# Dilated attention: router steps dealt over the heads, row copies on ScalarE, contexts in halves, the second router's root by Newton steps

## The reference, cut to what matters

```python
# dilated attention: 16 heads of 8 channels; segments of 256, 512 and the last 16 tokens,
# with dilation 1, 2, 4 (a head sees every r-th token of its segment in a Hilbert order)
s = einsum('bhqd,bhkd->bhqk', qd, kd) * SCALE;  p = softmax(s);  od = einsum('bhqk,bhkd->bhqd', p, vd)
t = t + o @ w_out + b_out
# the last mixture: routing on the layer-normed token
x = (t - mean) / sqrt(var + 1e-5);  gate_logits = x @ gate_weight.T
top_vals, top_idx = top_k(gate_logits, 2);  routing_w = softmax(top_vals)
# h_sum per expert, h_mean, y_mean = h_mean @ w2;  out = sum_k routing_w * y_mean[top_idx]
```

## Time and profile before

| | |
|---|---|
| median of the runs | 3198.56 us (3 runs, 3196.73 to 3207.51) |
| profiled execution | 3192.41 us, span 3190.6 us |
| busy over the span | PE 2720.5 us (85%), DVE 2120.3 (66%), ACT 1553.2 (49%), POOL 996.4 (31%) |
| mean granted TensorE clock | 0.92 |
| dilated stage, scores and finish | from 2040 us (first score) to 2822 us of the span |

### The profile page before, as it was taken

One profiled execution on the slowest core, in us unless ns is written; L12 is line 12 of the kernel. 1 busy time (PEld: TensorE's weight loads), 2 busy tenths in 40 slices (PEclk: granted clock), 3 DMA queues, 4 the chain that ended last, 5 costly groups with the idle time before them and its releaser, 6 DMA issues. The chain is left out here.

```text
span 3190.6 us, 63614 instructions
## 1 busy us (share of the span) xinstructions
PE 2720.5 (85%) x21060; PEld 1483.0 (46%) x21061; DVE 2120.3 (66%) x3976; ACT 1553.2 (49%) x3278; POOL 996.4 (31%) x1323
## 2 busy tenths in 40 slices
PE   8988799999999999999399889688888888728887
PEld 4545143333333434333299768354555554413334
DVE  6745777877777777774222268767777777646665
ACT  2246366666666666666155434444544444404442
POOL 0024011222222222222333474235655655630000
PEclk9989599999999999999699989788898898859998
DMA  2036522322223222220222234433232232032223
GB/s 87 1 122 228 80 38 41 57 47 43 43 48 53 52 43 43 44 43 9 90 62 62 69 121 159 100 54 60 59 65 60 59 65 60 24 121 61 60 59 118
DMA packets 209456, 215.90 MB, mean 68 GB/s; under 512 B 33280, under 2 KB 185152, under 8 KB 209216
## 3 DMA queue, kind: packets, MB, share of 16 engines
q1 hardware_dynamic: 180880, 175.22, 23.8%
q0 software_dynamic: 14336, 25.72, 3.0%
q10 hardware_dynamic: 14000, 11.73, 1.3%
HBM read 129.23 MB, written 81.90 MB: 66 GB/s over the span
## 5 line engine op out<-in xcount | busy, mean ns | idle before, releaser
L1544 ACT ACTIVATE attn_exps<-attn_sbank 128x392 f32<-128x392 f32 x1600 | 704.8, 504 | 466.3 <-PE attn_sbank L1461 461.5
L1589 DVE TENSOR_REDUCE attn_mx<-attn_rot 128x1 f32<-128x784 f32 x768 | 722.1, 967 | 187.4 <-PE attn_rot L1474 184.3
L2315 ACT ACTIVATE dil_exps<-dil_sbank 128x512 f32<-128x512 f32 x512 | 289.4, 598 | 364.4 <-PE dil_sbank L2213 361.2
L1474 PE MATMUL attn_rot<-attn_k,attn_q 96*128 96x392 bf16 x1536 | 402.0, 345 | 71.1 <-DVE attn_mx L1589 40.5
L1461 PE MATMUL attn_sbank<-attn_q,attn_k 99*128 99x392 bf16 x1536 | 450.5, 333 | 11.0 <-ACT attn_exps L1544 9.7
L2371 DVE TENSOR_REDUCE dil_mx<-dil_rot 128x4 f32<-128x1024 f32 x256 | 307.5, 1218 | 72.9 <-PE dil_rot L2223 70.7
L1501 PE MATMUL attn_acc<-attn_exps,attn_v 128*32 128x392 f32 x3584 | 349.8, 501 | 0.0
L1461 PEld LDWEIGHTS attn_sbank<-attn_q,attn_k 99*128 99x128 bf16 x1536 | 148.9, 98 | 269.3 <-ACT attn_exps L1544 134.7
L2704 PE MATMUL silu_ph<-silu_route_w,silu_xT 128*128 x424 | 238.2, 646 | 37.6 <-DVE silu_xT L2754 19.2
L1474 PEld LDWEIGHTS attn_rot<-attn_k,attn_q 96*128 96x128 bf16 x1536 | 117.8, 99 | 277.6 <-DVE attn_mx L1589 180.4
L2223 PE MATMUL dil_rot<-dil_k,dil_q 96*128 96x256 bf16 x1024 | 176.5, 302 | 75.5 <-DVE dil_mx L2371 49.5
(11 more groups left out here) (389 smaller groups left out, 4517.8 us busy)
## 6 DMA issues: line engine op xcount, KB each, us to landing
attn_q<-q_pieces SPq DMA_DIRECT2D x192, 98.0 KB, 3.5
attn_k<-k_pieces SPq DMA_DIRECT2D x192, 98.0 KB, 4.7
silu_x<-silu_rows SPq DMA_DIRECT2D x212, 64.0 KB, 1.7
dil_q<-dil_q_pieces SPq DMA_DIRECT2D x192, 66.0 KB
dil_k<-dil_k_pieces SPq DMA_DIRECT2D x192, 66.0 KB
q_pieces<-qkv_piece SPq DMA_DIRECT2D x16, 588.0 KB, 3.1
k_pieces<-qkv_piece SPq DMA_DIRECT2D x16, 588.0 KB, 4.2
v_rows<-qkv_v SPq DMA_DIRECT2D x16, 476.0 KB, 3.8
```

The source lines that it names most:

```text
L1474: ins = nc.tensor.matmul(rot[b][:, hf, 0:HS], q[nxt.side][g][0:QROWS, j, c * P:(c + 1) * P], k_[nxt.side][g][0:QROWS, j, cols], start=True ...
L1544: nc.scalar.activation(e_[:, n % NP, :], sbank[(n + t.side) % 3][:, 0:HS], ACT.Exp, scale=A_DIM ** -0.5).then_inc(s_ex, 1)
L1589: nc.vector.tensor_reduce(into, rot[b][:, :, 0:HS], AX.XY, ALU.max).then_inc(s_free, 1)
L2315: nc.scalar.activation(e_[:, k % NP, :], sbank[k % 3][:], ACT.Exp, scale=D_DIM ** -0.5).then_inc(s_ex, 1)
```

## The change

- Root: `act_root`, its square root on ACT and the reciprocal go; the two-picks router calls `dve_rsqrt`, as the first router does (a shift, a scaled negative, a first guess and three Newton rounds of three instructions, 12 on 112x7). The picks become 15 steps: in each, one step of the search for the best two and one of the norm go out together, after a wait for both of the step before.
- Copies: rows and gate are copied out of PSUM by ACT (`act_rows`, `act_gate`), as steps in ACT's list.
- `s_free` becomes one semaphore for each of the two `rot` banks, since two engines free them now.
- Contexts: `weigh` is dealt in halves (group, segment), 16 products each, at score units 8g+6 and 8g+10; `take` at 8g+12 (from 8g+13). An exponential that reuses a slot waits for the half that read it.
- Order: picks 0 to 9 at heads 11 to 15, two a head; picks 10 to 14 at heads 0 to 2 of the next turn (lag 2); ranks and soft at 3; places over heads 4 to 9; gate 10, store 11; scatters at heads 7 to 15 (2, 2, 1, 2, 1, 2, 1, 2, 1), at the end of a head; compact 3, den 5, add 7, rows 9; turn 0 at 10. POOL's norm comes at pick 13, in head 1 of the next turn.

```diff
-        self.ROOT = 2 + 2 + 3 * NEWTON if K == 1 else 9
-        self.PICKS = self.ROOT + 8 if K == 1 else 16
+        self.RSQRT = 2 + 3 * NEWTON
+        self.ROOT = 2 + self.RSQRT if K == 1 else 2 + self.RSQRT
+        self.PICKS = self.ROOT + 8 if K == 1 else self.ROOT + 2
...
+    def act_rows(self, act, im, rot):
+        nc, E = self.nc, self.ex.n
+        im.wait(act, self.s_xt, lambda e: e)
+        im.wait(act, self.s_cs, lambda e: self.PLACE_LINKS * (e - 1) + 4 if e else 0)
+        nc.scalar.activation(self.xc[:, 0:4, :], rot[0:TOK, 0, :].rearrange("k (c d) -> k c d", c=4), ACT.Copy)
+        nc.scalar.activation(self.xc[:, 4:NCH, :], rot[0:TOK, 1, 0:3 * P].rearrange("k (c d) -> k c d", c=3), ACT.Copy).then_inc(self.s_xc, 1)
+        return nc.scalar.activation(self.raw[:], rot[0:TOK, 1, 3 * P:3 * P + NCH * E].rearrange("k (c e) -> k c e", e=E), ACT.Copy)
...
     def dve_picks_two(self, dve, im):
+        ch = Links(dve, self.s_ch, self.PICK_LINKS * im.e, self.PICK_LINKS)
+        two, norm = self.dve_best_two(ch), self.dve_norm(dve, im, ch)
+        for n in range(self.ROOT + 1):
+            if n > 0:
+                ch.ready()
+            if n < 12:
+                next(two)
+            if n > 0:
+                next(norm)
+            yield
+        ch.ready()
+        dve.wait_ge(self.s_rs, im.e + 1)
+        self.nc.vector.tensor_tensor(self.df[:, :, 0], self.gap[:], self.rstd[:], ALU.mult).then_inc(self.s_df, 1)
...
-                dve.wait_ge(self.s_std, im.e + 1)
-                nc.vector.reciprocal(self.rstd[:], self.std[:]).then_inc(self.s_rs, 1)
...
-    def act_root(self, act, im):
-        act.wait_ge(self.s_var, im.e + 1)
-        self.nc.scalar.activation(self.std[:], self.var[:], ACT.Sqrt).then_inc(self.s_std, 1)
+    def dve_norm(self, dve, im, ch):
+        dve.wait_ge(self.s_sq, im.e + 1)
+        ch.link(nc.vector.tensor_reduce(self.total[:], self.xt[im.side][:], AX.X, ALU.add))
+        yield
+        ch.link(nc.vector.tensor_scalar(self.var[:], self.total[:], 1.0 / P, 1e-5, ALU.mult, ALU.add))
         yield
+        yield from self.dve_rsqrt(ch)
...
-    def dve_gate(self, dve, im, rot):
+    def act_gate(self, act, im, rot):
...
-            ins = self.nc.vector.tensor_copy(self.turned[:, 4 * TOK * b:4 * TOK * b + cs * TOK], rot[0:self.ex.n, b, 0:cs * TOK])
+            ins = self.nc.scalar.activation(self.turned[:, 4 * TOK * b:4 * TOK * b + cs * TOK], rot[0:self.ex.n, b, 0:cs * TOK], ACT.Copy)
...
+    PICKS_LATE = 10
+    PLACES_AT = {4: (0, 1), 5: (2, 3), 6: (4, 5), 7: (6,), 8: (7, 8), 9: (9, 10)}
+    SCATTERS_AT = {7: 2, 8: 2, 9: 1, 10: 2, 11: 1, 12: 2, 13: 1, 14: 2, 15: 1}
+
+    def late_steps(h, lag):
+        out = [("pick", n, lag) for n in range(PICKS_LATE, 15) if (n - PICKS_LATE) // 2 == h]
+        if h == 3:
+            out += [("ranks", lag), ("soft", lag)]
+        out += [("place", n, lag) for n in PLACES_AT.get(h, ())]
+        return out + {10: [("gate", lag)], 11: [("store", lag)]}.get(h, [])
...
-                if (exps and 8 * gr + 10 == n) or (finish and 8 * gr + 10 - D_UN == n):
-                    out.append(("weigh", gr))
-                if (exps and 8 * gr + 13 == n) or (finish and 8 * gr + 13 - D_UN == n):
+                for seg in range(2):
+                    at = 8 * gr + 6 + 4 * seg
+                    if (exps and at == n) or (finish and at - D_UN == n):
+                        out.append(("weigh", gr, seg))
+                if (exps and 8 * gr + 12 == n) or (finish and 8 * gr + 12 - D_UN == n):
                     out.append(("take", gr))
...
+                out += {3: [("compact",)], 5: [("den",)], 7: [("add",)], 9: [("rows",)]}.get(h, [])
+                out += [("pick", n, 1) for n in range(PICKS_LATE) if 11 + n // 2 == h]
+            if exps:
+                out += {2: [("turn", 1)], 5: [("score16",)], 7: [("exp16",)], 8: [("load", 0)], 10: [("weigh16",)], 15: [("load", 1)]}.get(h, [])
+            if maxima:
+                out += {6: [("max16",)], 10: [("turn", 0)]}.get(h, [])
+            if older:
+                out += scatter_steps(h, 2)
...
-            if k % 8 == 0:
-                t.wait(act, s_av, lambda e: 4 * e + k // 8 - 1)
+            if k % 4 == 0:
+                t.wait(act, s_av, lambda e: 8 * e + k // 4 - 3)
...
+                        if x[0] == "rows":
+                            act.wait_ge(s_fill, pos + 1)
+                            router.act_rows(act, im, rot[b]).then_inc(s_free[b], 1)
+                        if x[0] == "gate":
+                            act.wait_ge(s_fill, pos + 1)
+                            router.act_gate(act, im, rot[b]).then_inc(s_free[b], 1)
```

More of the change, by code:

```diff
@@ L763, in __init__ @@
         self.rstd = m.sb("r_rstd", [TOK, NCH])
+        self.bits = m.sb("r_bits", [TOK, NCH], i32)
+        self.half = m.sb("r_minus_half_var", [TOK, NCH])
+        self.root = [m.sb(f"r_root{n}", [TOK, NCH]) for n in two]
+        self.prod = [m.sb(f"r_root_product{n}", [TOK, NCH]) for n in two]
         if K == 1:
             self.lg = m.sb("r_lg", [TOK, NCH, E])
[L766 to L769, removed]
         else:
-            self.std = m.sb("r_std", [TOK, NCH])
             self.gap = m.sb("r_gap", [TOK, NCH])
@@ L879, in dve_picks_one @@
         yield
-        yield from self.dve_rsqrt(dve, ch)
+        root = self.dve_rsqrt(ch)
+        for n in range(self.RSQRT):
+            ch.ready()
+            next(root)
+            yield
         dve.wait_ge(self.s_rs, im.e + 1)
@@ L1951, in dilated_attention, with scatter_steps @@
     GROUPS = 4
[L1953 to L1961, removed]
-        return out + {4: [("gate", lag)], 5: [("store", lag)]}.get(h, [])
+    PICKS_LATE = 10
[7 more added lines that the diff above has]
+        return out + {10: [("gate", lag)], 11: [("store", lag)]}.get(h, [])
+    def scatter_steps(h, lag):
+        before = sum(c for k, c in SCATTERS_AT.items() if k < h)
+        return [("scatter", before + n, lag) for n in range(SCATTERS_AT.get(h, 0))]
     def steps(finish, exps, maxima, older):
@@ L1981, in steps @@
             score(2 * h + 1)
-            if maxima and h == 9:
-                out.append(("turn", 0))
-            if exps and h == 2:
-                out.append(("turn", 1))
-            if maxima and h == 6:
-                out.append(("max16",))
             if older:
-                out += route_steps(h, 2)
+                out += late_steps(h, 2)
             if finish:
-                out += {4: [("compact",)], 6: [("den",)], 9: [("add",)], 11: [("rows",)]}.get(h, [])
-                out += [("pick", n) for n in range(16) if 11 + (n + 2) // 4 == h] + [("root",)] * (h == 12)
+                out += {3: [("compact",)], 5: [("den",)], 7: [("add",)], 9: [("rows",)]}.get(h, [])
[6 more added lines that the diff above has]
+                out += scatter_steps(h, 2)
             if older and not exps and h == D_HEADS - 1:
                 for n in range(D_HEADS):
-                    out += [x for x in route_steps(n, 1) if x[0] != "scatter"]
-            if exps:
-                out += {5: [("score16",)], 7: [("exp16",)], 8: [("load", 0)], 10: [("weigh16",)], 15: [("load", 1)]}.get(h, [])
+                    out += late_steps(n, 1)
         return out
     pipe = Pipeline(steps, ("max", "max16", "turn", "compact", "den", "score16", "weigh16", "add", "rows", "ranks", "gate"), B, True)
-    ROUTE_STEPS = ("ranks", "soft", "place", "gate", "store", "scatter")
+    ROUTE_STEPS = ("pick", "ranks", "soft", "place", "gate", "store", "scatter")
     def image_of(t, x):
-        late = (x[0] in ("weigh", "take") and x[1] == 3) or x[0] in ("compact", "den", "add", "rows", "pick", "root")
+        late = x in (("weigh", 3, 1), ("take", 3)) or x[0] in ("compact", "den", "add", "rows")
         return t.plus(-x[-1] if x[0] in ROUTE_STEPS else -1 if late else 0)
@@ L2066, in dilated_attention @@
         s_fill = m.sem("rot_filled")
-        s_free = m.sem("rot_free")
+        s_free = [m.sem(f"rot_free{b}") for b in two]
         s_sc = m.sem("scores_ready")
@@ L2170, in do @@
                             router.pool_square(pool, im)
-                        if x == ("pick", router.ROOT):
+                        if x[:2] == ("pick", router.ROOT):
                             router.pool_norm(pool, im)
@@ L2359, in _ @@
                 router.dve_setup(dve)
+                picks, pos_rows = {}, {}
                 def do(t):
@@ L2363, in do @@
                     for (x, pos, b, lo) in pipe.turn(t):
+                        im = image_of(t, x)
                         if x[0] == "rows":
                             router.dve_router(dve, prv, rot[b])
-                        if lo is not None:
+                            picks[prv.e], pos_rows[prv.e] = router.dve_picks(dve, prv), pos
+                        if lo is not None and x[0] not in ("rows", "gate"):
                             if x[0] == "turn":
@@ L2411, in do @@
```

(4 more changed lines are left out.)

151 lines of the change are left out of this document (64 added, 87 removed).

## The result

The changed kernel takes 3148.39 us (median of 4 runs, 3142.3 to 3150.15) against 3197.64 for the kernel before in the same job: ratio 0.985, 95% interval 0.982 to 0.988. Faster by 49 us, where 75 were forecast. Its profiled execution took 3147.47 us (span 3145.0).

The account below looks back on a forecast made before the run. Each 47.9 us turn was held bound by DVE's burst, then PE's runs. DVE work 34.0, idle 8.2 and clock 0.8 gave 43.0; thirteen turns 62, turn 1 4, end 9, sum 75: forecast 3122 us, range 3060 to 3185.

Parts of the forecast that it names:

- the likeliest case: Whole kernel: forecast 3122 us from a turn of 43.0 us, own range 3095 to 3150; chance 52%.
- DVE's work in a turn: Dilated attention stage: 36.3 us less copies, reciprocal and POOL interference, plus 1.2 for Newton steps, gives 34.0.
- DVE also loses less to POOL: Second router's steps slowed beside POOL: 0.9 us gained a turn, ends 0 and 1.7; caught Newton products could cost 0.8.
- DVE's idle: Per turn 8.2 us: rows and gate 4.0, head 3 2.9, POOL's last split 0.7, rest 0.6; now 11.5.
- rival A: Fully dealt: DVE's idle falls to 5, turn 39.5, 122 us saved, 3075 us; chance 20%.
- The halves: Context weighings: 16 products where 32 stood, no added work; DVE's 4.2 us wait for maxima's products falls to some 1.5.
- Row and gate copies on ACT: Copies out of PSUM leave DVE: 1.4 + 1.0 us less a turn; ACT takes them at 1.3 and 1.0.
- The end: Turn 15 and tail: gate wait and root stall go, 9 us saved; 0 if POOL's late scatters eat it, 12 at most.
- Turn 1: Second image's turn, with root and row copies but no places or scatters: 4 of its 45.6 us saved.
- Rival B: Clock and port eat the gain: more half-clock stretches, picks caught by POOL; turn 46, 33 us saved, 3164; chance 15%.
- Rival C: POOL becomes the bound if its 25 to 27 us stretch reaches 33; slower, 3210 us and up; chance 6%.
- Rival D: The stall moves from the root to the copies in ACT's queue; turn 47 to 48, 3190 to 3200; chance 7%.

Follow-up runs that it names:

- e1: Changed kernel, but POOL takes context group 2's product and sum together with group 3's, four heads later in its order; 3096.9 us.
- e4: Changed kernel with the second router's root back on ACT as a square root, reciprocal on DVE; 3134.9 us.
- e12: Kernel before the change with only the Newton root added, 15 picks in heads 11 to 15; 3239.4 us.
- e7: e1 with the row and gate copies back on DVE; 3103.7 us.
- after: The kernel with the whole change, against the kernel before; 3148.4 us, ratio 0.982 to 0.988.
- e8: e1 with each context group's weighing whole again instead of in halves; 3136.9 us.
- e2: Changed kernel with six of an image's fourteen scatters put off to heads 3 to 5 of the next turn; 3096.5 us.
- e5: e1 with POOL kept as late as in the changed kernel, but writing constants instead of reading contexts; 3144.3 us.
- e9: Changed kernel with head 14's two scatters moved behind POOL's last split, so the split comes sooner; 3147.6 us.
- e11: e1 with head 14's two scatters moved behind POOL's last split; 3116.7 us.

## Why the prediction was right, and where its sizes were off

The mechanism held: a turn of 44.1 us (41 to 45 forecast), DVE's burst opened, no table load beside the scores, scatters back to back from head 7, POOL's last split 7.2 us into the next turn (8 forecast), DVE's longest single waits in the chain of rows and gate (1.83 us, behind the rows' products) and at compact (1.79). The median of 3148 lies in the likeliest case's own range of 3095 to 3150, at its slow end.

That the turn came within 1.1 us of the 43.0 is luck in part, for two errors pull against each other. The meeting with POOL costs 3.5 us a turn (44.1 against 40.6 in e1), which the sum had at nothing; the rest of the sum was 2.4 us too long (43.0 against e1's 40.6): 1.6 of it in DVE's work and 0.7 in its idle, by the turn of e1 shown (32.4 and 8.3). The terms:

- **What gave the gain.** Not the root: with it on ACT (e4) 62 us are saved, and by Newton's steps alone (e12) the kernel is 41 slower. Nor the copies, 0.6 us a turn (e7). What is left is the dealing, with the halves; the dealing was not run by itself, so that is argued by what remains.
- **DVE's work in a turn.** Forecast 34.0, measured 34.9. The term that failed is the port's: "DVE also loses less to POOL", a gain of 0.9. The picks did get free, but two Newton steps were caught and lost 2.4 us. The prediction knew that they could be caught and priced it at 0.8, outside its sum.
- **DVE's idle.** Forecast 8.2 and 0.8 for the clock, 9.0; measured 9.5 in after and 8.3 in e1. So the head-by-head estimate of the idle was good; what it lacked was PE's 2.1 us wait and the half clock behind it. Taken out (e1), the turn is 40.6, near rival A's 39.5, though not by A's way: DVE's work is lower there, its idle is not 5.
- **The halves.** DVE's waits for the maxima's products were to fall from 4.2 us to some 1.5; they are 6.2 in the turn shown (5.2 in e1), the longest 1.8 where it was 2.4. That part of the sum did not come, and no run shows what the halves are worth (e8).
- **Adding up work.** The sum took each microsecond off DVE as one off the turn. e7 shows that it isn't: 2.2 us of copies put back cost 0.6 a turn, since DVE's waits for the maxima's products fall from 5.2 to 2.8. "Row and gate copies on ACT" was sized about right as work (2.4) and about four times too high as time.
- **The end.** 9 us were forecast, nothing came, by the cause named beside it: POOL's late scatters (e2, where they are out of the way, has 9.8).
- **Turn 1** gave 6.2 for 4, and turn 2, one of the thirteen, 9.0: POOL has no scatters in turn 1, so it isn't late at the start of turn 2, and no step is caught there. The stage began 7.9 us later in this one profile.
- **Rival B** was at work in part: steps caught by POOL and the clock behind them, at 1.1 us a turn over the forecast where it had 3, with 8.5 us at half clock, under the 12 that it asks for.
- **Rival C.** POOL as a bound was given 6 of 100. The stretch that it counted at 25 to 27 us takes 26.5 (the two splits, 2404.23 to 2430.71). In after PE waits for the split in one turn alone (1.44 us, turn 12), but it is 1 us away in the others (split done at 2430.71, product at 2431.68), and in e5 PE waits for it in every turn from turn 3 on.
- **Rival D** is out: PE waits 0.34 and 0.65 us for ACT's copies, not more. ACT waits 2.5 us for the rows' products, but has no score ready meanwhile: PE makes the next one at 2410.34, and ACT's copy begins at 2410.53.
- **Slips of the sum.** The upper end of 47.5 comes to 47.2 (34.0 + 11.5 + 0.8 + 0.9), the smaller waits to 2.8 us, not 2 (11.5 less the four named), 3117 and 6 to 3123. None moves the forecast.

By the Trainium skill, SBUF — State Buffer, "Who interferes with whom", a VectorE instruction with two SBUF inputs contends with a GpSimd one that reads SBUF, and not with one that only writes it. These runs agree on both: 1.47 us beside the context product, 0.16 beside the constants.

## What to carry to other kernels

When small two-input steps are dealt over a loop on DVE, draw POOL's queue beside them: a step of 7 columns beside a context product or sum ended only with it here, and as a maximum behind it feeds PE, 2 us of wait cost 3.5 us of a turn. Moving the POOL instruction was enough: taking one sum four heads later gave as much (51 us) as the whole change (49); moving the step was not tried. And where two waits end at nearly the same time, take both away before calling either harmless; the removal of one gave 4 us or none here (e5, e9), of both 51 (e1). A move can also make a new meeting, as e9 and e11 did: read the length of each small step again after it.

## What the runs showed of the hardware that was not expected

- One 7-column DVE instruction waited out two POOL instructions in a row: 3.06 us for the norm of 1.69 and the product of 1.04 (e11), 2.56 in e8. Where it started 0.97 us after the norm, it ended with the norm alone (0.74 in after).
- A held step can start before the POOL instruction whose end it shares: 0.39 us before the context product in after (2423.84 against 2424.23), 0.34 before the norm in e11. Why stays open.
- POOL's scatters by themselves hold up no such step: in e1 they stand back to back beside the Newton steps, none of which lasts over 0.18 us.
- With a wait of PE of 2.0 to 2.7 us near a turn's start the granted clock stood at 0.5 for 6.8 or 10.2 us of the turn in after, for 10.2 in all turns of e5 from turn 3 on but one (3.4 in turn 12, with a wait of 3.7), for 6.8 to 13.7 in e9; in e1, where PE waits 1.4 us at most, for 3.4 us in most turns.
